# Attention with its row maxima taken by halves of the queries, and the chunk stream 48 instead of 80 chunks ahead

## What is computed

```python
att = jnp.einsum('bhqd,bhkd->bhqk', q, k) * (1.0 / math.sqrt(HD))      # first attention: no mask
att = jax.nn.softmax(att, axis=-1)
y = jnp.einsum('bhqk,bhkd->bhqd', att, v)
...
attn = jnp.einsum('bhqd,bhkd->bhqk', q, k) / math.sqrt(HEAD_DIM)       # second attention
attn = attn + alibi_bias(seq_len, N_HEADS)[None] + causal_mask(seq_len)[None, None]
attn = jax.nn.softmax(attn, axis=-1)
```

## Time and profile before

| | us |
|---|---|
| median of 3 timed runs | 2952.81 (2951.69 to 2960.51) |
| the profiled execution | 2950.72 |
| its span, first to last instruction | 2948.9 |
| PE busy | 2667.6 (90%) |
| DVE busy | 1946.6 (66%) |
| ACT busy | 1261.4 (43%) |
| POOL busy | 657.1 (22%) |
| chunks' reductions, L1776 on DVE | 1031.0 in 1792 instructions |
| chunks' products, L1517 on PE | 597.0 in 1792 |
| units' products, L1574 on PE | 510.7 in 1792 |
| value products, L1589 on PE | 442.3 in 3584 |
| exponentials, L1653 on ACT | 794.8 in 896 |

### The profile page before, as it was taken

How to read it: one execution, slowest core, us unless ns; L and a number is a source line. 1 busy time by engine, 2 the same in 40 slices (tenths; PEclk the granted TensorE clock), 3 DMA queues, 4 the chain that set the end, 5 groups by cost and what they waited for, 6 DMA issues and landing times. The chain is left out here.

```text
span 2948.9 us, 40309 instructions
## 1 busy us (share of the span) xinstructions
PE 2667.6 (90%) x14292; PEld 1275.0 (43%) x14292; DVE 1946.6 (66%) x4227; ACT 1261.4 (43%) x1901; POOL 657.1 (22%) x640
## 2 busy tenths in 40 slices
PE   3987999999999999797999995999999999798997
PEld 2442233333333332354455663454544454455564
DVE  5877878777877885585774334767677674576333
ACT  1432456556655667443211221355455556221221
POOL 0554122131230300153002441222121100001341
PEclk8996899999999999998999997799999999899998
DMA  3004330321303300001202663633233430301566
GB/s 118 1 1 101 49 60 12 54 50 22 60 17 49 58 8 1 1 1 61 92 33 49 137 135 85 129 64 57 45 61 54 66 50 2 107 33 33 122 138 166
DMA packets 163075, 175.78 MB, mean 60 GB/s; under 512 B 19570, under 2 KB 136242, under 8 KB 162738
## 3 DMA queue, kind: packets, MB, share of 16 engines
q1 hardware_dynamic: 145348, 150.48, 22.9%
q0 software_dynamic: 12416, 17.84, 3.8%
q10 hardware_dynamic: 5120, 4.98, 0.5%
HBM read 116.32 MB, written 56.13 MB: 58 GB/s over the span
## 5 line engine op out<-in xcount | busy, mean ns | idle before, releaser
L1776 DVE TENSOR_REDUCE a_mx<-a_bank 128x1 f32<-128x512 f32 (+3 forms) x1792 | 1031.0, 627 | 285.3 <-PE a_bank L1517 219.0
L1653 ACT ACTIVATE a_E<-a_bank 128x1024 f32<-128x1024 f32 (+3 forms) x896 | 794.8, 932 | 477.5 <-PE a_bank L1574 328.3
L1517 PE MATMUL a_bank<-a_KT,a_QT 96*128 96x512 bf16 (+4 forms) x1792 | 597.0, 379 | 35.1 <-DVE a_mx L1776 25.2
L1574 PE MATMUL a_bank<-a_QT,a_KT 99*128 99x512 bf16 (+4 forms) x1792 | 510.7, 360 | 18.5 <-DMA a_QT<-a_mT 16.0
L1589 PE MATMUL a_bank<-a_E,a_Vg 128*32 128x512 f32 (+3 forms) x3584 | 442.3, 566 | 0.7 <-ACT a_E L1653 0.7
L1517 PEld LDWEIGHTS a_bank<-a_KT,a_QT 96*128 96x128 bf16 (+1 forms) x1792 | 152.2, 98 | 526.1 <-DVE a_mx L1776 305.6
L1574 PEld LDWEIGHTS a_bank<-a_QT,a_KT 99*128 99x128 bf16 (+1 forms) x1792 | 170.4, 99 | 199.0 <-ACT a_E L1653 37.0
L848 PE MATMUL d_bank<-wdT,d_hT 128*128 128x256 f32 (+1 forms) x768 | 201.9, 407 | 21.7 <-DVE x L1054 21.7
L960 ACT ACTIVATE d_silu<-d_bank 128x512 f32<-128x512 f32 x96 | 57.2, 596 | 375.6 <-PE d_bank L835 368.4
L1044 DVE SCALAR_TENSOR_TENSOR d_silu<-d_silu,d_bank 128x512 f32<-128x512 f32 x96 | 65.6, 683 | 227.3 <-ACT d_silu L960 219.9
L433 POOL TENSOR_TENSOR f_hl<-f_hT,f_hh 128x512 f16<-128x512 f32 x96 | 111.1, 1157 | 392.1 <-ACT f_hh L452 392.1
(11 more groups left out here) (234 smaller groups left out, 3537.8 us busy)
## 6 DMA issues: line engine op xcount, KB each, us to landing
parts<-a_parts SPq DMA_DIRECT2D x64, 384.0 KB, 2.5
a_QT<-parts SPq DMA_DIRECT2D x180, 128.0 KB, 5.4
a_KT<-parts SPq DMA_DIRECT2D x180, 128.0 KB, 8.0
d_wgu<-in_L_ffn_w_gate SPq DMA_DIRECT2D x64, 176.0 KB
d_wgu<-in_L_ffn_w_up SPq DMA_DIRECT2D x64, 176.0 KB
d_wd<-in_L_ffn_w_down SPq DMA_DIRECT2D x64, 176.0 KB
normalised<-d_xn SPq DMA_DIRECT2D x8, 1152.0 KB, 4.7
acc<-d_zero SPq DMA_DIRECT2D x66, 128.0 KB, 1.8
```

Source lines behind the costliest of these rows:

```text
L1517: last = nc.tensor.matmul(out[:, 0:w], QT[0:W, h, qt * P:(qt + 1) * P], KT[0:W, h, kh * HALF:kh * HALF + w], start=True, stop=not diag)
L1574: last = nc.tensor.matmul(out, KT[:, h, kt * P:(kt + 1) * P], QT[:, h, half * HALF + c0:(half + 1) * HALF], start=True, stop=not diag)
L1653: nc.scalar.activation(E[:, u % 2, 2 * pair:2 * pair + 2, c0:HALF], bank[:, 2 * pair:2 * pair + 2, c0:HALF], ACT.Exp).then_inc(exps, 1)
L1776: nc.vector.tensor_reduce(mx[:, j, qt, kh:kh + 1], out[:, 0:w], AX.X, ALU.max).then_inc(freed_dve, 1)
```

## The change

- `maxima`, `turn_m` and `rows` are done for one half of the queries at a time, 32 instead of 16 of them in a phase, each over half the elements (`m`, `mrest`, `mparts`, `mT` shrink to half). `rows` still issues four DMAs, each of half the size.
- The chunks of a group's first half of the queries are FIRST = 32 in the first attention and 16 in the second. The opening now has `AHEAD` chunks: 48 in the first attention and 44 in the second.
- `m_units` replaces `m_unit`: (4, 12) in the first attention, (1, 5) in the second. The first entry is for the second half of the group that is running, the second for the first half of the next group. `turn_m` stands two units later: at 6 and 14, and at 3 and 7.
- TensorE waits for rows at the start of each half: at units 0 and 8 in the first attention, and at units 0 and 4 in the second.
- A load's place in the SP queue gets one more lower bound, unit `m_units[1] + 3` of the group in which its last projection stands. In the first attention load(b, 0) moves from unit 13 to 15 by it; the other loads of both phases keep their places relative to the units.

```diff
-    AHEAD = 4 * C // U
-    m_unit = next(u for u in range(U) if AHEAD + C * u // U >= C)
+    FIRST = sum(qt < KPH for _, qt, _, _ in chunks)
+    AHEAD = 44 if second else 48
+    m_units = [next(u for u in range(U) if AHEAD + C * u // U >= ready) for ready in (C, C + FIRST)]
...
-    opening = ahead_of_rows + some(0, C + 3) + [("turn_m", 0)] + some(C + 3, C + AHEAD)
+    opening = ahead_of_rows + some(0, FIRST + 3) + [("turn_m", 0)] + some(FIRST + 3, AHEAD)
...
-    beside = {(n // U, n % U): some(C + AHEAD + C * n // U, C + AHEAD + C * (n + 1) // U) for n in range(BG * U)}
+    beside = {(n // U, n % U): some(AHEAD + C * n // U, AHEAD + C * (n + 1) // U) for n in range(BG * U)}
...
+        beside[G, m_units[0] + 2].insert(0, ("turn_m", 2 * G + 1))
         if G + 1 < BG:
-            beside[G, m_unit + 2].insert(0, ("turn_m", G + 1))
+            beside[G, m_units[1] + 2].insert(0, ("turn_m", 2 * G + 2))
...
-                def rows(G):
-
-                    sp.wait_ge(mT_kept, START + G + 1)
+                def rows(q):
+
+                    G, half = q // QH, q % QH
+                    sp.wait_ge(mT_kept, START + q + 1)
                     for j in range(GH):
-                        dst = QT[W:WM, G % NG * GH + j, :].rearrange("r (q c) -> r q c", c=P)
-                        sp.dma_start(dst, mT[j * 3 * TPB:(j + 1) * 3 * TPB, :]).then_inc(m_rows, 16)
+                        dst = QT[W:WM, G % NG * GH + j, half * HALF:(half + 1) * HALF].rearrange("r (q c) -> r q c", c=P)
+                        sp.dma_start(dst, mT[j * 3 * KPH:(j + 1) * 3 * KPH, :]).then_inc(m_rows, 16)
...
-                todo = [(G * U + m_unit + 2, rows, (G + 1,)) for G in range(BG - 1)]
+                todo = [(G * U + m_units[h] + 2, rows, (2 * G + h + 1,)) for G in range(BG) for h in range(QH) if 2 * G + h + 1 < QH * BG]
...
-                        todo.append((max(G * U + u + 5, ((b - 1) * NG + g + 1) * U), load, (b, g)))
+                        todo.append((max(G * U + u + 5, ((b - 1) * NG + g + 1) * U, G * U + m_units[1] + 3), load, (b, g)))
...
                 for G in range(BG):
-                    pe.wait_ge(m_rows, START + (G + 1) * GH * 16)
                     for u in range(U):
+                        if u == 0 or units[u][0] != units[u - 1][0]:
+                            pe.wait_ge(m_rows, START + (QH * G + units[u][0] + 1) * GH * 16)
                         score_pair(G, u, 0)
...
-                        if u == m_unit and G + 1 < BG:
-                            maxima(G + 1)
+                        if u == m_units[0]:
+                            maxima(2 * G + 1)
+                        if u == m_units[1] and G + 1 < BG:
+                            maxima(2 * G + 2)
```

More of the change, by code:

```diff
@@ L1321, in attention_phase @@
         mx = sb(tag + "mx", [P, GH, TPB, 2])
[L1322 to L1325, removed]
+        m = sb(tag + "m", [P, GH, KPH])
+        mrest = sb(tag + "mrest", [P, GH, KPH])
+        mparts = sb(tag + "mparts", [P, GH, 3, KPH], BF16)
+        mT = sb(tag + "mT", [GH * 3 * KPH, P], BF16)
         yT = sb(tag + "yT", [P, 2, KC, 2 * P])
@@ L1522, in fill @@
                         pe.wait_ge(m_step, START + (x[1] + 1) * 5)
-                        last = nc.tensor.transpose(out[0:GH * 3 * TPB].bitcast(BF16)[:, 0:P],
+                        last = nc.tensor.transpose(out[0:GH * 3 * KPH].bitcast(BF16)[:, 0:P],
                                                    mparts[:].rearrange("p j r q -> p (j r q)"), ident_b[:])
@@ L1752, in maxima @@
                 def maxima(G):
-                    dve.wait_ge(freed_dve, freed_at(("chunk", (G + 1) * C - 1)))
+                    half = G % QH
+                    dve.wait_ge(freed_dve, freed_at(("chunk", G // QH * C + (C if half else FIRST) - 1)))
                     if G:
                         dve.wait_ge(filled, START + place["turn_m", G - 1] + 1)
-                    nc.vector.tensor_reduce(m[:], mx[:], AX.X, ALU.max).then_inc(m_step, 1)
+                    nc.vector.tensor_reduce(m[:], mx[:, :, half * KPH:(half + 1) * KPH], AX.X, ALU.max).then_inc(m_step, 1)
                     dve.wait_ge(m_step, START + G * 5 + 1)
@@ L1778, in take @@
                         dve.wait_ge(m_rows, START + x[1] * GH * 16)
-                        nc.vector.tensor_copy(mT[:], out[0:GH * 3 * TPB].bitcast(BF16)[:, 0:P]).then_inc(mT_kept, 1)
+                        nc.vector.tensor_copy(mT[:], out[0:GH * 3 * KPH].bitcast(BF16)[:, 0:P]).then_inc(mT_kept, 1)
                         dve.wait_ge(mT_kept, START + x[1] + 1)
@@ L1837, in _ @@
                     take(x)
-                    if x == ("chunk", C - 1):
+                    if x == ("chunk", FIRST - 1):
                         maxima(0)
```

## The result

The changed kernel takes 3046.07 us (median of 4 runs, 3042.05 to 3051.84), the kernel before 2954.39 in the same comparison (4 runs): 1.031 times as long, 95% interval 1.028 to 1.033. The span of the profiled execution is 3041.6 us, against 2948.9: 92.7 us more. The prediction had the direction and the main mechanism, with 59 us. The time is 14 us above its upper bound, and two terms of its sum came out above the upper bounds that it gave them: the price of the added chains and the low clock.

A forecast was written before the change was run, and what follows sets the result against it. TensorE was taken as the bound inside the stream, so its waits count in full. A −16.7 us and B +75.9 us, with 83 us of waits at unit 4, made +59 us: 3012 us, range 2966 to 3032.

The forecast's parts named there:

- The mechanism that decides: B, unit 4: rows turned at unit 3 come late; chain 4.98 us against 1.93 of work, plain groups wait 3.0.
- The openings: Fewer chunks ahead of the first score: gain 19.2 us in A (at least 17) and 9.6 us in B.
- The gate in A: Loads put behind the rows in groups 1, 5 and 9 of A: gain 12.7 us, waits and low clock together.
- Not effective: Rival: the added bound does not move the loads in A either; 12.7 us more, 3025 us; chance 0.03.
- the price of a chain: 16 more maxima chains per phase: 0.54 us each in A (8.6), 0.3 in B (4.8); bounds together 3 and 19.
- tail: End of each phase, where the chunk stream now ends later: loss 6.6 us in A and 4.1 us in B.
- row waits of before: B, group to group: rows turned at unit 7 instead of 10, so 6.4 us of TensorE waits (8 waits) vanish.
- the clock's term: Low clock behind 13 waits of 3 us or more at unit 4 of B: 1.0 us each, 13 us, bounds 0 and 20.
- Queued behind both: B, groups 4, 8, 12: unit 3's rows queue behind load(b, 2) and load(b, 3); 12 us wait each, 36 us.
- Short waits only: Rival: rows overtake loads in groups 4, 8, 12 of B and the clock holds through 3 us; 2972 us; chance 0.21.
- Faster: Rival: half-sized rows land fast enough that unit 4 of B does not wait; −24 us, 2929 us; chance 0.06.
- Heavier: Rival: longer low clock per wait, and rows in groups 2, 6, 10 of B also behind loads; 3037 us; chance 0.07.

The follow-up runs named there:

- e1: Changed kernel with the transposition of the maxima in B one unit after them instead of two: 3008.06 us, ratio 1.020.
- e2: Changed kernel with load(b, 2) and load(b, 3) of B sorted behind the row transfers of unit 3: 3012.57 us, ratio 1.021.
- e10: e3 with load(0, 2), load(0, 3) and load(b, 1) of B also put behind the half's rows: 2956.36 us, ratio 1.0017.
- e3: Changed kernel with both edits, the earlier transposition of e1 and the later loads of e2: 2969.51 us, ratio 1.006.
- e4: Kernel before with only the added lower bound on a load's place: 2940.35 us, ratio 0.9967.
- e5: Kernel before with e4's bound and, in B, the transposition one unit after the maxima, no halves: 2929.54 us, ratio 0.992.
- e9: e3 without three of the five VectorE operations of each maxima chain (second and third bf16 parts left zero): 2934.96 us, ratio 0.993.
- e7: Changed kernel with useless TensorE products before the row wait at unit 4 of B, 50 in groups 4, 8, 12, else 12: 3026.79 us, ratio 1.025.
- e8: Changed kernel with the unit 3 row transfers of groups 4, 8, 12 of B issued on ScalarE's queue: 3051.3 us, ratio 1.035.
- e6: Changed kernel with AHEAD 80 in A and 48 in B, and loads behind the rows as in e2: 3021.88 us, ratio 1.023.

## Why the prediction was right, and where it was not

- **The mechanism that decides was right, and right in size.** Chain 5.03 us (4.98 predicted), wait in a plain group 2.99 (3.0), groups 4, 8 and 12 together 39.6 (36), all waits at unit 4 75.7 (70.4). e1 and e2 each removed one of its two parts. Of the 5.3 us too few, 2.6 are group 0, counted as plain: load(0, 2) and load(0, 3) stand ahead of its rows. e10 moved them, and the wait of 6.51 in e3 went to 0.47.
- **The openings.** A gained 17.5 us (55.0 to 37.6; 19.2 predicted, at least 17), B 8.6 (9.6), by the first value product. The first rows were no obstacle.
- **The gate in A.** Predicted 12.7; e4 shows 12.7 in the trace and 9 in the timed runs. "Not effective" falls.
- **The first step that failed: the price of a chain.** "Half as many elements will save little" was right. 0.54 us for one more chain in A and "In B VectorE has more room, and I take 0.3 each" were not: 13.4 us in all, at most 19, where the traces show about 30.
  - In A the gains of 17.5 and 12.7, less the net 11.1, leave 19.1 us for chains and tail, where 15.2 stood. Groups 14 and 15 hold the tail; they take 7.7 us more than before, 5.9 without two chains of 0.88. So 13.2 us remain, 0.8 a chain. The clock hides some of it, since it loses less in after (6.8 us) than in e4 (11.9): at equal clock groups 0 to 13 take 15.5 us more than in e5, 1.1 each. It is no fixed price, but 0.5 in groups 2, 5, 6, 8 and 10, 0.9 in group 13 and 2.8 to 3.1 in groups 3, 7 and 11.
  - In B 43.3 us have to be shared among chains, tail and clock: 103.5 + 8.6 for the opening − 75.7 of waits + 6.9 for the row waits of before (636.9 in before, 630.0 in e5). The traces allow two ways. Groups 0 to 13 of after, less their row waits and 0.85 of their lost clock, take 15.0 us more than those of e5: 1.1 each, 17.1 for 16 chains, and groups 14 and 15 leave 1.4 for the tail. Groups 0 to 13 of e10, less its wait of 0.47 and a stretch of low clock in group 8 (1.6), take 17.2 more: 1.2 each, 19.7, and 2.5 for the tail. Either is about four times the 4.8 that I took for the chains; the tail is smaller than my 4.1.
  - The error was to price a chain by what a plain group of A had left over, 1.6 us shared out among three items, and to scale it by VectorE's idle share. e9 shows that in B this idle share is not what matters: three of its operations give back only 0.14. In e10 0.84 of it lie where two transpositions share a unit; how the rest is made up was not settled.
- **The second step that failed: the size of the clock's term.** 13 us taken, bounds 0 to 20. B loses 29.1 us of clock outside the waits, and at the 0.85 that the comparison with e7 gives, this is an estimated 24.8 us. Less the 22.2 of e10 for chains and tail, the 43.3 leave 21.1. Thirteen waits at 1.0 us each was too little: fourteen waits are of 2 us and more, and in e7's comparison most cost 1.3 to 1.6, two cost 2.3 and 2.9, and one nothing.
- **"Queued behind both" was the wrong picture with the right number.** That the rows share SP's queue is not what makes them late: e8 gave them another one and they waited as long. e2 shows that it is the loads ahead of them.
- **Rivals.** "Short waits only" fell twice, with waits of 12.67, 11.80 and 15.08 and with a clock of 0.60. "Faster" needed a chain of 3.4 us and the chain is 5.03. "Heavier" was nearest in its total (3037) and for the wrong reason in part: groups 2, 6 and 10 wait 4.1 us together where the forecast had 3.9, but the clock did cost more.
- **The range.** With the terms as read from after the sum is 59 + 16.9 (chains 30.3 for 13.4) + 11.8 (clock 24.8 for 13) + 5.3 (waits) + 2.7 (openings) − 3.4 (tail 7.3 for 10.7) − 0.5 (row waits of before) = 91.8, beside 92.7. That it closes proves little, since in either phase one term is what the others leave; the shares of chains and clock in B are good to some 4 us. Of the gap of 33.7 us half are the chains and a third the clock. The range ended at 3032, 20 us above the sum, and these two took 28.7.

## What to carry to other kernels

On an engine that takes its work in order, put the producer at least the whole measured latency of its chain ahead of the consumer before splitting a step into halves: here 5 us of chain had 2 us of cover, and one unit more was worth 33 us. Splitting also doubles the fixed price of the chain, which halves of the data don't reduce; with all waits cured the halves still cost 27 us against the version with whole groups, a later load and an earlier transposition (e5, 2929.5 us). A small urgent transfer should be issued before the bulk transfers, since here another queue didn't let it past them. And two traces of one kernel can differ by several us through the clock alone (3.4 to 10.2 us of lost clock in the same A), so it should be read before a small difference is explained.

## What the runs showed of the hardware

- Four transfers of 3.0 KB issued on an otherwise empty queue moved no packet for 5.7 us (2067.1 to 2072.8) while another queue's loads kept the sixteen DMA engines full (e8).
- VectorE operations of 0.17 us took 1.12 to 1.28 us beside GpSimd's operations on 128x512 f32, and TensorE stood 3.77 us for it (e6).
- Halving the elements of a chain changes little. The first is before, the others after (mean ns behind the busy time):

```profile
L1761 DVE SCALAR_TENSOR_TENSOR a_mrest<-a_m,a_mparts 128x32 f32<-128x32 f32 x32 | 8.8, 274 | 1.1
```
```profile
L1766 DVE SCALAR_TENSOR_TENSOR a_mrest<-a_m,a_mparts 128x16 f32<-128x16 f32 x64 | 17.8, 278 | 2.2
L1771 DVE TENSOR_TENSOR a_mparts<-a_mrest,a_mparts 128x16 bf16<-128x16 f32 x64 | 14.9, 233 | 2.2
```

- More work made the kernel faster: useless products during the waits took 12.2 us off eight groups through the clock (e7).
- The clock fell behind 20 of 24 waits of TensorE of 2.5 to 3 us (after, e2, e8), and in group 4 behind a wait of 1.70 us in e4 but not in before.
